# Attention scores from two float32r parts instead of three bf16 parts, for two heads at a time in 64-row halves of the array, with the loop written out

## What is computed

```
x = layer_norm(hidden, ln1_g, ln1_b)
q, k, v = jnp.split(x @ c_attn_w + c_attn_b, 3, axis=-1)
a = attention(q, k, v, causal)                 # softmax(q k^T / 4) v for each head
hidden = hidden + a @ attn_proj_w + attn_proj_b
x = layer_norm(hidden, lnx_g, lnx_b)
q = x @ q_attn_w + q_attn_b
k, v = jnp.split(ctx @ x_kv_w + x_kv_b, 2, axis=-1)
a = attention(q, k, v, scorer_logits, lower triangle and two diagonals above it)
hidden = hidden + a @ x_proj_w + x_proj_b
h = gelu(layer_norm(hidden, ln2_g, ln2_b) @ fc_w + fc_b)
hidden = hidden + h @ mlp_proj_w + mlp_proj_b
```

## Time and profile before

| | |
|---|---|
| median of 3 runs | 1320.84 us (1320.83 to 1323.61) |
| profiled execution: its own time | 1324.19 us |
| its span | 1322.5 us |
| mean granted TensorE clock | 0.933 |
| PE busy | 1116.2 us, 84% |
| DVE busy | 786.8 us, 59% |
| ACT busy | 614.5 us, 46% |
| POOL busy | 434.6 us, 33% |

### The profile page before, as it was taken

The page is one execution under the profiler, slowest core; times in us unless marked ns, Lnnn a source line. Parts: engine busy times, 40 slices in busy tenths (PEclk is TensorE's granted clock), DMA queues, the critical chain, the costliest instruction groups (busy, mean ns, idle before and its releaser), DMA issues.

```text
span 1322.5 us, 22082 instructions
## 1 busy us (share of the span) xinstructions
PE 1116.2 (84%) x7360; PEld 670.9 (51%) x7360; DVE 786.8 (59%) x1898; ACT 614.5 (46%) x1154; POOL 434.6 (33%) x805
## 2 busy tenths in 40 slices
PE   4394775888989999889989799899989999948967
PEld 2142442545455655556455555566456645534635
DVE  3471663576776677656767577667756677417513
ACT  1052242454664457444655357445744475505433
POOL 3041151243424342423524242434323243403220
PEclk9587796889999999999999899999989999988989
DMA  9406344908063543626081533626090800080000
GB/s 222 56 19 77 52 52 61 114 17 98 16 85 49 75 52 44 90 40 88 2 111 27 78 46 44 90 39 88 13 116 10 105 17 1 10 103 2 17 0 17
DMA packets 50391, 74.11 MB, mean 56 GB/s; under 512 B 6472, under 2 KB 24808, under 8 KB 50281
## 3 DMA queue, kind: packets, MB, share of 16 engines
q1 hardware_dynamic: 50281, 72.68, 40.0%
HBM read 17.45 MB, written 4.19 MB: 16 GB/s over the span
## 4 chain that ended last, share of the span: by engine, by line
PE 59%; issue 14%; DVE 10%; DMA 9%; ACT 6%; POOL 2%; SPq 1%; DVEq 0%; ACTq 0%; POOLq 0%
PE dense L515 14%; PE dense L521 12%; PE pv_out L588 10%; PE scores L574 8%; PE max_scores L556 7%; DVE row_max L789 5%; PE dense L509 3%; PE max_scores L559 3%; DMA q_stack_cross<-max_rows 3%; DMA q_stack_self<-parts_q 3%; DMA q_stack_self<-max_rows 2%; ACT probs L679 2%; DVE rest_k L822 1%; PE dense L611 1%; ACT inner L704 1%
## 5 line engine op out<-in xcount | busy, mean ns | idle before, releaser
L679 ACT ACTIVATE probs<-scores 128x512 f32<-128x512 f32 (+3 forms) x768 | 383.4, 529 | 455.7 <-PE scores L574 451.3
L789 DVE TENSOR_REDUCE row_max<-max_scores 128x1 f32<-128x512 f32 (+6 forms) x1024 | 445.6, 482 | 238.5 <-PE max_scores L559 233.9
L946 POOL TENSOR_SCALAR_AFFINE_SELECT probs<-probs 128x256 f32<-128x256 f32 x512 | 210.0, 430 | 464.1 <-ACT probs L679 463.3
L556 PE MATMUL max_scores<-k_stack_self,q_stack_self 96*128 96x512 bf16 (+3 forms) x512 | 148.7, 319 | 72.2 <-issue 56.0
L556 PE MATMUL max_scores<-k_stack_cross,q_stack_cross 99*128 99x512 bf16 (+3 forms) x512 | 145.8, 312 | 38.0 <-issue 31.7
L574 PE MATMUL scores<-q_stack_cross,k_stack_cross 101*128 101x512 bf16 (+3 forms) x512 | 135.4, 308 | 31.2 <-DMA q_stack_cross<-max_rows 19.6
L574 PE MATMUL scores<-q_stack_self,k_stack_self 98*128 98x512 bf16 (+3 forms) x512 | 137.1, 310 | 17.5 <-ACT probs L679 10.0
L521 PE MATMUL dense<-mlp_w,inner 128*128 128x256 f32 x512 | 127.7, 396 | 8.5 <-DVE rest_k L822 5.0
L515 PE MATMUL dense<-feat_b,fc_w 128*128 128x512 f32 x256 | 124.1, 610 | 3.0 <-ACT rest_k L713 1.1
L521 PEld LDWEIGHTS dense<-mlp_w,inner 128*128 128x128 f32 x512 | 97.5, 196 | 28.4 <-DVE rest_k L822 6.5
L556 PEld LDWEIGHTS max_scores<-k_stack_self,q_stack_self 96*128 96x128 bf16 x512 | 51.7, 101 | 108.9 <-issue 68.1
(11 more groups left out here) (95 smaller groups left out, 1500.7 us busy)
## 6 DMA issues: line engine op xcount, KB each, us to landing
q_stack_self<-parts_q SPq DMA_DIRECT2D x48, 256.0 KB, 9.5
k_stack_self<-parts_k SPq DMA_DIRECT2D x48, 256.0 KB, 15.5
q_stack_cross<-parts_q SPq DMA_DIRECT2D x48, 256.0 KB, 9.0
k_stack_cross<-parts_k SPq DMA_DIRECT2D x48, 256.0 KB, 12.7
x_in<-in_x SPq DMA_DIRECT2D x8, 512.0 KB, 10.7
x_in<-in_ctx SPq DMA_DIRECT2D x8, 512.0 KB, 10.4
hidden<-in_x SPq DMA_DIRECT2D x8, 512.0 KB, 13.4
out_y<-hidden SPq DMA_DIRECT2D x32, 128.0 KB, 1.7
```

Source lines behind the costliest of these rows:

```text
L556: pe.matmul(max_scores[:, bank, c0:c0 + W[q]], q_stack[at.kind][0:rows_, head, q * P:(q + 1) * P], k_stack[at.kind][0:rows_, head, 0:W[q]] ...
L679: nc.scalar.activation(probs[:, head % (2 * GH), c0:c0 + w], scores[:, part % EXP_BANKS, 0:w], ACT.Exp, scale=SCALE).then_inc(exp_done, 1)
L789: last = nc.vector.tensor_reduce(row_max[:, g % 2, c:c + 1], max_scores[:, part % MAX_BANKS, c0:c0 + W[q]], AX.X, ALU.max)
L946: nc.gpsimd.affine_select(out=v, in_=v, compare_op=ALU.is_ge, fill=0.0, base=q0 - kb * P + LAST[at.kind], pattern=[[0, 2], [1, P]], channe ...
```

## The change

It has three parts.

- **Parts of q and k.** They are float32r now, and two instead of three. The stacks have three blocks of 16 rows (48 rows for self, 50 for cross, and two more in S). ACT writes the first part, DVE the second; the second DVE instruction and that of POOL are gone. Each DMA moves as many bytes as before, and there are still six for q and six for k.
- **Pairs of heads.** The stacks hold one head of a pair on partitions 0 to 63 and the other on 64 to 127. M and S stand only in even beats, for both heads: each tile is made by two matmuls, one in each half, into two PSUM banks. The mask is made by one more bf16 matmul in each half (`step_q`, `step_k`). M of a pair waits until the first tile of the pair before has been read, S of a pair until both exponentials of the pair before are done. The row maxima are turned by a float32 matmul (L602), split by DVE after it (L786, L788) and taken to the stack by four DMAs instead of one (L483).
- **The loop is written out**: all eleven rounds of the list stand one after the other.

Beside this, two of the four temporary buffers of the GELU, which lay in `rest`, are one new buffer that is used twice, so the square of the third and fourth pair of blocks in ACT waits for y (L867) of the pair two before.

```diff
-STACK = 6 * HD
+STACK = 3 * HD
 LAST = {"self": 0, "cross": 2}
-KMAX = {"self": STACK, "cross": STACK + 3}
+KMAX = {"self": STACK, "cross": STACK + 2}
 KALL = {kind: KMAX[kind] + 2 for kind in KMAX}
 
-PARTS = {"q": (0, 1, 0, 1, 2, 0), "k": (0, 0, 1, 1, 0, 2)}
+PARTS = {"q": (0, 1, 0), "k": (0, 0, 1)}
+HALF = P // 2
...
-FIRST, LOOP_FROM, LOOP_TO, END = -1, 3, NB - 2, NB + 2
+FIRST, END = -1, NB + 2
...
-                if what in "MS":
+                if what in "MS" and beat % 2 == 0:
...
-        parts = {s: sb(f"parts_{s}", [P, 3, HC, T], BF16) for s in "qk"}
-        rest = {s: sb(f"rest_{s}", [P, HC, T]) for s in "qk"}
...
+        parts = {s: sb(f"parts_{s}", [P, 2, HC, T], F32R) for s in "qk"}
+        gelu_more = sb("gelu_more", [P, 2, T])
+        gelu_temp = 2 * [normed[:].rearrange("p t h -> p (t h)").rearrange("p (c t) -> p c t", t=T), gelu_more[:]]
+
+        q_stack = {k: sb(f"q_stack_{k}", [P, NH // 2, T], F32R) for k in KALL}
+        k_stack = {k: sb(f"k_stack_{k}", [P, NH // 2, T], F32R) for k in KALL}
...
-            for like in range(FIRST, LOOP_FROM):
+            for like in range(FIRST, END):
...
-                body(LOOP_FROM, i)
-            for like in range(LOOP_TO, END):
-                body(like, like)
...
-                        for p_, ready in ((0, hi), (1, mid), (2, lo)):
+                        for p_, ready in ((0, hi), (1, lo)):
                             if ready is not hi or kind == "self":
                                 sp.wait_ge(ready[name], (b + 1) * HC)
                             for r, which in enumerate(PARTS[name[0]]):
-                                if which == p_:
-                                    sp.dma_start(dst[r * HD:(r + 1) * HD, :, :],
-                                                 src[:, p_].rearrange("p c t -> p (c t)")).then_inc(stack_loaded[name], 16)
+                                for c in range(HC):
+                                    if which == p_:
+                                        row0 = c * HALF + r * HD
+                                        sp.dma_start(dst[row0:row0 + HD, :, :].bitcast(F32),
+                                                     src[:, p_, c].bitcast(F32)).then_inc(stack_loaded[name], 16)
                     if name == "MT":
-                        sp.wait_ge(max_rows_ready, at.n * NG + g + 1)
-                        sp.dma_start(q_stack[at.kind][KMAX[at.kind]:KALL[at.kind], g * GH:(g + 1) * GH, :],
-                                     max_rows[:]).then_inc(max_loaded, 16)
+                        pairs, n = slice(g * GH // 2, (g + 1) * GH // 2), GH * TB // 2
+                        for r, (ready, rows_) in enumerate(((max_hi_ready, max_hi), (max_lo_ready, max_lo))):
+                            sp.wait_ge(ready, at.n * NG + g + 1)
+                            for half in range(2):
+                                row0 = half * HALF + KMAX[at.kind] + r
+                                sp.dma_start(q_stack[at.kind][row0:row0 + 1, pairs, :].bitcast(F32),
+                                             rows_[half * n:(half + 1) * n, :].bitcast(F32)).then_inc(max_loaded, 16)
...
-                        wait(pe, max_scores_read, at.n * BEATS + part + 1 - MAX_BANKS)
+                        wait(pe, max_scores_read, at.n * BEATS + part + 2 - MAX_BANKS)
                         c0 = 0
                         for q in MAX_TILES[r]:
-                            pe.matmul(max_scores[:, bank, c0:c0 + W[q]],
-                                      q_stack[at.kind][0:rows_, head, q * P:(q + 1) * P],
-                                      k_stack[at.kind][0:rows_, head, 0:W[q]], start=True, stop=False)
-                            last = pe.matmul(max_scores[:, bank, c0 + q * P:c0 + W[q]], ident_b[:],
-                                             mask_of(at.kind, q), start=False, stop=True)
+                            for half in range(2):
+                                rows_ = slice(half * HALF, half * HALF + KMAX[at.kind])
+                                pe.matmul(max_scores[:, (part + half) % MAX_BANKS, c0:c0 + W[q]],
+                                          q_stack[at.kind][rows_, pair, q * P:(q + 1) * P],
+                                          k_stack[at.kind][rows_, pair, 0:W[q]], start=True, stop=False)
+                            for half in range(2):
+                                last = pe.matmul(max_scores[:, (part + half) % MAX_BANKS, c0 + q * P:c0 + W[q]],
+                                                 step_q[half * HALF:(half + 1) * HALF, :],
+                                                 mask_of(at.kind, q, half), start=False, stop=True)
...
-                            pe.wait_ge(max_loaded, (at.n * NG + g + 1) * 16)
+                            pe.wait_ge(max_loaded, (at.n * NG + g + 1) * 4 * 16)
+
+                        wait(pe, exp_done, at.n * BEATS + part + 2 - EXP_BANKS)
...
                             _, q0, w = prob_cols(at.kind)[kb]
-                            last = pe.matmul(scores[:, part % EXP_BANKS, c0:c0 + w],
-                                             k_stack[at.kind][0:rows_, head, kb * P:(kb + 1) * P],
-                                             q_stack[at.kind][0:rows_, head, q0:T], start=True, stop=True)
+                            for half in range(2):
+                                rows_ = slice(half * HALF, half * HALF + KALL[at.kind])
+                                last = pe.matmul(scores[:, (part + half) % EXP_BANKS, c0:c0 + w],
+                                                 k_stack[at.kind][rows_, pair, kb * P:(kb + 1) * P],
+                                                 q_stack[at.kind][rows_, pair, q0:T], start=True, stop=True)
...
-                        pe.wait_ge(max_split, at.n * NG + g + 1)
-                        last = pe.transpose(d.bitcast(BF16)[:, 0:P], max_parts[:], ident_b[:])
+                        pe.wait_ge(max_scores_read, at.n * BEATS + (g + 1) * GT)
+                        last = pe.matmul(d[0:GH * TB, 0:P], row_max[:, g % 2, :], ident[:], start=True, stop=True)
...
-                            wait(act, gelu_ready, b * PAIRS + (pair == 3))
-                            if pair in (1, 2):
-                                for n in "12":
-                                    wait(act, lo["qk"[pair - 1] + n], seen("qk"[pair - 1] + n))
+                            wait(act, gelu_ready, b * PAIRS + max(pair - 1, 0))
...
-                        wait(dve, max_loaded, (at.n * NG + g) * 16)
-                        nc.vector.tensor_copy(max_rows[:], d.bitcast(BF16)[0:2 * GH * TB, 0:P]).then_inc(max_rows_ready, 1)
+                        wait(dve, max_loaded, (at.n * NG + g) * 4 * 16)
+                        top = d[0:GH * TB, 0:P]
+                        nc.vector.tensor_copy(max_hi[:], top).then_inc(max_hi_ready, 1)
+                        dve.wait_ge(max_hi_ready, at.n * NG + g + 1)
+                        nc.vector.tensor_tensor(max_lo[:], top, max_hi[:].bitcast(F32), ALU.subtract).then_inc(max_lo_ready, 1)
...
-                        dve.wait_ge(hi[name], n)
-                        nc.vector.scalar_tensor_tensor(out=rest[name[0]][:, part, :], in0=d, scalar=column(name, part),
-                                                       in1=parts[name[0]][:, 0, part, :], op0=ALU.add,
-                                                       op1=ALU.subtract).then_inc(remains[name], 1)
-                        dve.wait_ge(remains[name], n)
-                        nc.vector.tensor_copy(parts[name[0]][:, 1, part, :], rest[name[0]][:, part, :]).then_inc(mid[name], 1)
+                        dve.wait_ge(hi[name], b * HC + part + 1)
+                        both = parts[name[0]]
+                        nc.vector.scalar_tensor_tensor(out=both[:, 1, part, :], in0=d, scalar=column(name, part),
+                                                       in1=both[:, 0, part, :].bitcast(F32), op0=ALU.add,
+                                                       op1=ALU.subtract).then_inc(lo[name], 1)
...
-                    elif name in lo:
-                        pool.wait_ge(mid[name], b * HC + part + 1)
-                        nc.gpsimd.tensor_tensor(parts[name[0]][:, 2, part, :], rest[name[0]][:, part, :],
-                                                parts[name[0]][:, 1, part, :], ALU.subtract).then_inc(lo[name], 1)```

On PE, inside an attention at a place where the row maxima of a group are turned, before (`mask_self` with `ident_b` is the mask, `ident_b` with `max_parts` is MT):

```order
L556 MATMUL max_scores<-k_stack_self,q_stack_self 128x512
L559 MATMUL max_scores<-mask_self,ident_b 128x128
L574 MATMUL scores<-q_stack_self,k_stack_self 128x512
L556 MATMUL max_scores<-k_stack_self,q_stack_self 128x384
L559 MATMUL max_scores<-mask_self,ident_b 128x128
L574 MATMUL scores<-q_stack_self,k_stack_self 128x384
L607 MATMUL dense<-ident_b,max_parts 128x128
L556 MATMUL max_scores<-k_stack_self,q_stack_self 128x256
```

207 lines of the change are left out of this document (92 added, 115 removed).

## The result

The changed kernel takes 1367.07 us (median of 4 runs, 1362.94 to 1367.9), the kernel before 1320.84 us (4 runs beside it, 1317.53 to 1323.61). The ratio is 1.034, with a 95% interval of 1.0318 to 1.0362. It is slower by 46 us, where I had forecast 30 us less: 76 us too low, and of the wrong sign.

What follows compares the result with a forecast made beforehand. The prediction took PE to bound the rounds and summed -157 + 54 + 10 + 40 + 28 + 16 - 10 - 11 = -30 us against the profiled 1324.2 us: 1294 us, or 1291 us for the median; range 1235 to 1355 us.

Steps and rivals of the forecast that it cites:

- What bounds the kernel: PE sets the pace in the rounds; before about 330 us it also idles for the first M of an attention.
- M and S afterwards: PE's M and S fall from 0.91 to 0.50 us a double beat, saving 157 us over 384 double beats.
- (1): PE turns between array halves and full array, 0.1 us each, 0.2 us a double beat with other work: +54 us.
- The rival of free turns: Turns between halves and the full array cost PE nothing: 1237 us (1225 to 1265), chance 0.20.
- (2): MT on PE becomes a float32 matmul, 0.15 us more in each of 64: +10 us.
- (3): S of a pair fills both banks, so PE waits for two exponentials in light double beats: +40 us (0 to 60).
- (5): M of a pair waits until DVE has read the previous pair's first bank: +16 us (0 to 50).
- (4): Row maxima go by four transfers; three more issues on SP's queue delay S: +28 us (0 to 50).
- (6): The last step of the parts goes on DVE and POOL, freeing the path mostly at the start: -10 us.
- (7): Writing out the loop removes two turns at 5.5 us where PE waits: -11 us.
- slower, by the banks: Rival: score buffers handed over in pairs couple PE to DVE and ACT: 1341 us (1325 to 1360), chance 0.20.
- my two bounds: M and S at 0.43 or 0.91 us a double beat; rival without overlap or with two-cycle columns: 1402 to 1448 us, chance 0.12.

Runs made afterwards that it cites:

- Experiment 7: The changed kernel with bf16 in place of float32r, two bf16 parts of q and k, coarser scores; 1237.64 us, ratio 0.9359.
- experiment 5: The kernel before, loop written out, its 1024 mask matmuls using only 64 array rows, so 2048 turns; 1449.37 us.
- experiment 2: The kernel before, loop written out, M and S in pairs waiting for two banks, still three bf16 parts, whole array, one row-maxima transfer; 1350.99 us.
- experiment 3: The bf16 pairs of experiment 2, but each head waits for its own bank and reports it alone; 1306.13 us.
- experiment 6: The changed kernel with each group's row maxima sent by two transfers instead of four; 1347.75 us.

## Why the prediction was wrong, step by step

- **What bounds the kernel** was right: PE in the rounds, the first M at the start.
- **M and S afterwards, 0.50 us a double beat, and 157 us saved by it: this is the step that failed.** "I take 0.50 us, near the lower end", I wrote, with pairs of weight loads that "must fit behind the tiles". Measured are 0.76 us, of which some 0.10 us are the way out of the halves: bf16 in halves needs 0.309 us for S of 512, where 0.213 us are columns, and only 0.23 us in the two places where M in halves follows it directly at the 2.4 GHz level. So the tiles took 0.66 us where I had 0.50 us, 0.16 x 384 = 61 us in all. Experiment 7 shows the cause is the type: the same tiles in bf16 take 0.55 - 0.10 = 0.45 us, close to my lower bound of 0.43 us. The extra 0.09 to 0.10 us of a float32r tile is the difference of the weight loads (medians of 183 and 93 ns). That the load is what doesn't hide is read from these rows; no run took the load away alone. The Trainium skill gives 128 columns of weights some 107 ns ("TensorE: Matmul & The Clock Gate", LDWEIGHTS). The bf16 load is near this, and the float32r load is not.
- **(1) Turns, +54 us**: right in kind, somewhat small. I had 0.1 us on the way in and 0.1 us on the way out, and both are there: the last float32 matmul of 512 columns before M takes 0.522 instead of 0.429 us (medians, in float32r; 0.525 us in bf16 halves), and 0.10 us stand in S. A third piece I didn't have: the first float32 matmul behind S takes 0.533 instead of 0.432 us, in float32r and bf16 alike. The way in shows in the changed kernel where four dense matmuls stand behind other dense work and before M. They take 1.82 us, and four at 0.429 us are 1.72 us:

```profile
657.77 1.88 PE L508 MATMUL dense<-feat_a,qkv_w 128*128 128x512 f32 x4
659.59 0.50 PE L548 MATMUL max_scores<-k_stack_self,q_stack_self 48*128 48x512 f32 x2
```

  In all it is some 32 us in S (0.10 us in the 321 places where other work follows it), 22 us before M and 16 us behind S: 70 us. The rival of free turns is refuted by this and by experiment 5.
- **(2) MT, +10 us**: not tried by itself. MT takes 0.31 us to the next tile (705.53 to 705.84 in the timeline above), where I had 0.07 us before and 0.15 us more. Over 64 groups the trace has 14.5 us more than in experiment 2, a turn to the halves among them.
- **(3) and (5), +40 and +16 us**: the mechanism is shown, by experiments 2 and 3, at 43 us for both. The place was wrong. I had put most of it in six light double beats of a round; experiment 2 has 9 us in the middle rounds and 32 of its 43 us before group 14, where M and DVE take turns at three banks with nothing else for PE to do.
- **(4) Four transfers, +28 us**: the size is borne out as far as it was tried, the place is not. Two fewer give 19 us, two thirds of 28, and the 3.81 us to S are near the 4.1 us that I had worked out; the third transfer was not taken away. But the waits of S for row maxima didn't grow: 26.4 us before, 17.4 us in the changed kernel, where my sign asked for more than 27 us. Of what experiment 6 saves, some 10 us are idle time of PE, and most of the rest is the same dense matmuls at a higher clock.
- **(6) -10 us**: DVE and POOL are less busy, by 52 and 66 us, but no row shows a place where PE gained from it. I count nothing.
- **(7) The loop, -11 us**: right, and somewhat small: 15 us.
- **The clock**: I had no term for it. The mean granted clock of the span fell from 0.933 to 0.906.

The chain of experiments says where the sum went wrong: 15 us less by the loop (I had 11), 43 us more by two banks at once (I had 56), and then 16 us more by float32r, halves, MT and transfers together, where my terms gave -157 + 54 + 10 + 28 - 10 = -75 us. So the last step is off by 91 us, and the other two make up for 17 us of it. For this step the next table adds up the distances between starts of PE's matmuls over the whole trace, with idle time (0.15 us and more before a start) apart:

| us | bf16 pairs (experiment 2) | changed kernel | more |
|---|---|---|---|
| M and S, masks included | 408.4 | 343.3 | -65 |
| MT | 7.6 | 22.1 | +14.5 |
| last dense matmul before M | 74.2 | 96.3 | +22 |
| first dense matmul behind S | 46.3 | 61.9 | +16 |
| other dense matmuls | 428.7 | 448.8 | +20 |
| PV | 160.5 | 163.9 | +3 |
| idle | 209.9 | 216.0 | +6 |

M and S give 65 us, or 97 us without the way out of the halves in S, where I had 157 us: this is by far the largest miss. The other dense matmuls are the same ones with the same medians at the 2.4 GHz level (0.109, 0.216 and 0.429 us); they are longer in sum because more of them run at the 1.2 GHz level: 56 us of their time instead of 19 us, and half of the 37 us between them is what the lower level costs. So the clock costs some 18 us in dense work alone.

Of my signs of being wrong, two came: a double beat's M and S take over 0.6 us (0.76 us), and the waits for DVE are above 60 us (70.6 us). The kernel was slower, then, by two rivals at once, each in part: "slower, by the banks" with its 43 us, and a float32r tile between my two bounds. I had given the first a chance of 0.20 and the second only at its full price, 1402 us and more.
